# Building the stacked queries and keys of an attention: copies on chip in place of a store and a read

## The reference

```
def _L0_xattn_ref(x1, x2, Wq, bq, Wk, bk, Wv, bv):
    q = proj(x1t, Wq, bq)        # 8 heads of 16 values, 512 positions
    k = proj(x2t, Wk, bk)
    v = proj(x2t, Wv, bv)
    scores = jnp.einsum('bhqd,bhkd->bhqk', q, k) / jnp.sqrt(16)
    attn = jax.nn.softmax(scores, axis=-1)
    out = jnp.einsum('bhqk,bhkd->bhqd', attn, v)
...
x = x + jnp.tanh(g_xattn[0]) * _L0_xattn_ref(_layernorm(x, axis=-1), ctx_2048, ...)
x = x + jnp.tanh(g_ffn[0]) * _L0_ffn_ref(_layernorm(x, axis=-1), ...)
```

## Time and profile before

| | us |
|---|---|
| median of 3 runs | 1391.8 |
| lowest and highest run | 1387.26, 1391.97 |
| the profiled execution, and its span | 1386.7, 1384.8 |
| attention turns, first exact scores to the last values | 51.84 to about 877 |

### The profile page before, as it was taken

One profiled execution on the slowest core, in us unless ns is written; L12 is line 12 of the kernel. 1 busy time (PEld: TensorE's weight loads), 2 busy tenths in 40 slices (PEclk: granted clock), 3 DMA queues, 4 the chain that ended last, 5 costly groups with the idle time before them and its releaser, 6 DMA issues.

```text
span 1384.8 us, 34397 instructions
## 1 busy us (share of the span) xinstructions
PE 1288.3 (93%) x12274; PEld 682.2 (49%) x12274; DVE 975.1 (70%) x1661; ACT 871.8 (63%) x1720; POOL 861.5 (62%) x1267
## 2 busy tenths in 40 slices
PE   2899999999999999999999989799999999999997
PEld 0233333333333333333333323587788888888886
DVE  5989889999999998989999877457654333333332
ACT  2488888888888888888888768333334333333332
POOL 8647777678787878877887643442114555555553
PEclk7799999999999999999999999999999999999999
DMA  7677887778888888788888773676555998885665
GB/s 187 185 197 227 224 241 220 207 227 214 201 223 207 213 218 227 191 222 210 218 217 221 162 185 90 161 161 149 127 175 105 214 216 193 178 189 110 108 110 81
DMA packets 167522, 256.65 MB, mean 185 GB/s; under 512 B 31717, under 2 KB 65132, under 8 KB 167358
## 3 DMA queue, kind: packets, MB, share of 16 engines
q1 hardware_dynamic: 149102, 217.08, 59.0%
q0 software_dynamic: 18256, 37.38, 14.9%
HBM read 141.06 MB, written 112.27 MB: 183 GB/s over the span
## 4 chain that ended last, share of the span: by engine, by line
PE 61%; DVE 12%; issue 10%; DMA 7%; POOL 3%; ACT 3%; SPq 2%; POOLq 1%; DVEq 0%; ACTq 0%
PE m_banks L956 21%; PE bank L913 12%; PE bank L882 10%; DVE row_max L1129 8%; PE m_banks L860 7%; PE bank L838 3%; PE bank L888 3%; DMA arena<-parts_q 2%; PE bank L844 2%; ACT arena L1413 2%; DMA arena<-ht_d 1%; POOL xs L780 1%; PE bank L978 1%; SPq L458 1%; PE bank L869 1%
## 5 line engine op out<-in xcount | busy, mean ns | idle before, releaser
L1129 DVE TENSOR_REDUCE row_max<-m_banks 128x2 f32<-128x1024 f32 x512 | 615.0, 1222 | 76.1 <-PE m_banks L860 67.9
L1413 ACT ACTIVATE arena<-bank 128x512 f32<-128x512 f32 x1024 | 552.4, 606 | 73.4 <-PE bank L882 71.9
L882 PE MATMUL bank<-arena 112*32 112x512 bf16 x4096 | 336.2, 382 | 6.6 <-ACT arena L1413 3.2
L913 PE MATMUL bank<-arena 128*32 128x512 f32 x2048 | 280.2, 598 | 0.4 <-ACT arena L1421 0.3
L882 PEld LDWEIGHTS bank<-arena 112*32 112x32 bf16 x4096 | 114.7, 95 | 266.0 <-ACT arena L1413 132.4
L792 POOL DMA_INDIRECT out<-xs,ids x71 | 112.3, 1582 | 173.4 <-ACT xs L1495 135.7
L860 PE MATMUL m_banks<-arena 48*128 48x512 bf16 x1024 | 177.4, 393 | 39.6 <-DVE row_max L1129 25.7
L956 PE MATMUL m_banks<-w_ring,h_hi 128*128 x568 | 183.0, 403 | 0.0
L1484 ACT ACTIVATE arena<-m_banks 128x256 f32<-128x256 f32 x103 | 39.5, 384 | 186.9 <-PE m_banks L956 186.9
L860 PEld LDWEIGHTS m_banks<-arena 48*128 48x128 bf16 x1024 | 40.4, 93 | 175.2 <-DVE row_max L1129 79.9
L1337 DVE TENSOR_TENSOR arena<-arena,m_banks 128x256 f32<-128x256 f32 x71 | 29.9, 421 | 116.5 <-ACT arena L1484 116.5
(11 more groups left out here) (182 smaller groups left out, 1999.9 us busy)
## 6 DMA issues: line engine op xcount, KB each, us to landing
arena<-parts_k SPq DMA_DIRECT2D x128, 192.0 KB
arena<-parts_q SPq DMA_DIRECT2D x128, 192.0 KB
parts_k<-arena SPq DMA_DIRECT2D x64, 256.0 KB, 6.6
parts_q<-arena SPq DMA_DIRECT2D x64, 256.0 KB, 5.1
pv_d<-arena SPq DMA_DIRECT2D x32, 512.0 KB, 4.3
split_d<-staged SPq DMA_DIRECT2D x30, 512.0 KB, 9.1
w_ring<-split_d SPq DMA_DIRECT2D x60, 256.0 KB, 3.9
arena<-in_w SPq DMA_DIRECT2D x36, 256.0 KB, 8.4
```

The lines of the kernel that those rows point to most:

```text
L882: last = nc.tensor.matmul(out[c, :], k_stack[b % 3][0:SHIFTED, h, kt * P + c.start:kt * P + c.stop], q_stack[b % 3][0:SHIFTED, h, :], star ...
L913: last = nc.tensor.matmul(pv_ps[2 * DH * j:2 * DH * (j + 1), :], v_ones[b % 3][:, kt, GROUP * g + j, :], probs[pair % 3][:, j, :], start=( ...
L1129: nc.vector.reduce_max(pair, m_ps[(STEPS * b + u) // 2 % M_PAIRS], AX_X).then_inc(s_mx, 1)
L1413: nc.scalar.activation(probs[group % 3][:, j, :], bank_of["scores", b, s], ACT.Exp, scale=float(DH) ** -0.5).then_inc(s_exp, 1)
```

## The change

`parts_d`, `write` and `read` are gone. `copy_parts(b, n, part)` copies one part from its tile straight into the stacks: in slot `at` of three, rows base+at, base+at+3, ... (16 partitions, 3 apart) of a stack receive one part of 16 values by 8 heads. Where both halves (`base` 0 and 64) hold the same part for all heads it is one transfer of 128 KB for each half; otherwise even and odd heads (`a`) differ, and it is transfers of 64 KB of four heads each. For one batch that is 10 transfers for keys (HI 4, MID 4, LO 2) and 8 for queries (HI 4, MID 2, LO 2), 6 of them whole. The two heads of a pair in `max_scores` are now neighbours (2j+a), and the reduction on DVE writes its two columns accordingly.

```diff
+SLOTS_OF = (((HI, HI), (HI, MID), (MID, LO)), ((HI, LO), (MID, MID), (HI, HI)))
+COPIES = tuple(sum(2 if first == second else 4 for first, second in slots) for slots in SLOTS_OF)
...
-        parts_d = [[dram(f"parts_{n}{i}", (4, DH, HEADS, L), BF16) for i in range(2)] for n in "kq"]
...
+            def copy_parts(b, n, part):
                 if part == HI:
+                    if n == 0:
+                        if b >= 3:
+                            sp.wait_ge(s_es, STEPS * (b - 2))
+                        if b < 3:
+                            sp.wait_ge(s_blank[b], 2)
                     sp.wait_ge(s_hi, 2 * b + n + 1)
+                if part == MID:
                     sp.wait_ge(s_part, 4 * b + 2 * n + 2)
+                stack, src = (k_stack, q_stack)[n][b % 3], parts[n][part]
+                for at, (first, second) in enumerate(SLOTS_OF[n]):
+                    for base in (0, LANE):
+                        rows = stack[base + at:base + at + STACK - 2:len(SLOTS_OF[n]), :, :]
+                        if part == first == second:
+                            sp.dma_start(rows, src).then_inc(s_cp[n], DMA)
+                        else:
+                            for a in range(2):
+                                if part == (first if base == LANE * a else second):
+                                    sp.dma_start(rows[:, a:HEADS:2, :], src[a:P:2, :]).then_inc(s_cp[n], DMA)
...
             for i in TURNS:
                 if is_b(i + 2):
-                    write(i + 2, 1, HI)
+                    copy_parts(i + 2, 0, HI)
                 if is_b(i):
                     row(i, 1)
...
                 if is_b(i + 2):
-                    if i + 2 > 0:
-                        read(i + 2, 0)
-                    write(i + 2, 1, MID)
-                    if i + 2 == 0:
-                        read(0, 0)
+                    copy_parts(i + 2, 0, MID)
+                    copy_parts(i + 2, 0, LO)
+                    for part in (HI, MID, LO):
+                        copy_parts(i + 2, 1, part)
...
-                if is_b(i + 2):
-                    read(i + 2, 1)
...
-                if is_b(i + 3):
-                    for part in (HI, MID):
-                        write(i + 3, 0, part)
...
# split (POOL) and evacuate (ACT) wait for s_cp[n] in place of s_wr[n]; max_scores (PE) for both s_cp
-                    pe.wait_ge(s_rd[b % 3], READS * DMA * (b // 3 + 1))
+                    for kind in range(2):
+                        pe.wait_ge(s_cp[kind], COPIES[kind] * DMA * (b + 1))
...
-                    rows, h = slice(LANE * a, LANE * a + STACK), GROUP * g + 2 * a + j
+                    rows, h = slice(LANE * a, LANE * a + STACK), GROUP * g + 2 * j + a
```

More of the change, by code:

```diff
@@ L147, in build @@
         held = [a.take(3 * L // 2, BF16).rearrange("p (t l) -> p t l", t=3) for _ in range(2)]
-        parts = [[held[n][:, HELD[n].index(part), :] for part in (HI, MID, LO)] for n in range(2)]
+        parts = [[held[n][:, part, :] for part in (HI, MID, LO)] for n in range(2)]
         wq, wk, wv = (a.take(P) for _ in range(3))
@@ L282, in build @@
         s_part = sem("s_part")
-        s_wr = [sem(f"s_wr{i}") for i in range(2)]
-        s_rd = [sem(f"s_rd{i}") for i in range(3)]
+        s_cp = [sem(f"s_cp{i}") for i in range(2)]
         s_ms = sem("s_ms")
@@ L395, in middle_rows @@
             return stack[LANE // 2:LANE, :, :].rearrange("p h l -> p (h l)").bitcast(F32)
-        def lane(v, a):
-            return v.rearrange("p (g a j) l -> p a g (j l)", g=2, a=2)[:, a, :, :]
         @block.sync
@@ L433, in _ @@
                 load_x(b)
-            def write(b, n, part):
-                if b >= 2 and part == HI:
-                    sp.wait_ge(s_rd[(b - 2) % 3], READS * DMA * ((b - 2) // 3 + 1))
+            def copy_parts(b, n, part):
                 if part == HI:
+                    if n == 0:
[3 more added lines that the diff above has]
+                            sp.wait_ge(s_blank[b], 2)
                     sp.wait_ge(s_hi, 2 * b + n + 1)
-                else:
+                if part == MID:
@@ L667, in split @@
                 pool.wait_ge(s_part, 4 * b + 2 * n)
-                pool.wait_ge(s_wr[n], WRITES * DMA * b)
+                pool.wait_ge(s_cp[n], COPIES[n] * DMA * b)
                 hi, mid, lo = parts[n]
@@ L1127, in maximum @@
                 half, w = divmod(u // 2, GROUP * KT // 2)
-                pair = row_max[b % 2][:, GROUP * KT * half:GROUP * KT * (half + 1)].rearrange("p (a w) -> p w a", a=2)[:, w, :]
+                pair = row_max[b % 2][:, GROUP * KT * half:GROUP * KT * (half + 1)].rearrange("p (j a t) -> p j t a", a=2, t=KT)[:, w // KT, w % KT, :]
                 nc.vector.reduce_max(pair, m_ps[(STEPS * b + u) // 2 % M_PAIRS], AX_X).then_inc(s_mx, 1)
@@ L1394, in evacuate @@
                         act_e.wait_ge(s_part, 4 * (b - 1) + 2 * n + 2)
-                        act_e.wait_ge(s_wr[n], WRITES * DMA * b)
+                        act_e.wait_ge(s_cp[n], COPIES[n] * DMA * b)
                     nc.scalar.activation(proj[n], bank_of["projection", b, n], ACT.Identity, bias=bias[:, n:n + 1]).then_inc(s_evac, 1)
```

## The result

The changed kernel takes 1400.7 us (median of 9 runs) where the kernel before takes 1392.0 beside it: a ratio of 1.0067, 95% interval 1.0038 to 1.0097 (the two medians alone give 1.0063). Forecast were 14 us less. A gain "on the changed kernel" is the quotient of two such ratios.

What follows compares the result with a forecast made beforehand. The prediction took a turn as a tight weave of PE, DVE and ACT, with PE idle time ending in transfers to win. Start 4, turns 10 and m_rows 0 made 14 us less: 1378 us against the median 1391.8, range 1362 to 1398.

Steps and rivals of the forecast that it cites:

- Start: Kernel's start: first maxima 6.4 us earlier, first exact scores from 51.84 to 47.5; 4 us gained, bounds 1 and 6.4.
- The stalls on `parts_q`: In the turns: ten stalls of the maxima's scores waiting for query parts end; 10.0 us gained.
- Issue of the copies: SP's queue: 0.62 us a copy, 18 copies 11.2 us, 3.8 us more each turn, covered by SP's own waits.
- that rival: SP becomes the bound: copies cost over 0.86 us to issue, PE starts turns late; 1417 us at 0.95; chance 0.12.
- The wait for the reciprocals: SP's queue: the reciprocals' load directly follows their store, a new wait of 2.5 us a turn.
- `m_rows`: Exact scores' waits for the rows of maxima, 3.9 us before: taken as 0 change, bounds gain 3.9 and loss 5.
- DMA engines: DMA share of a turn falls from 0.85 to 0.69 by bytes; no gain booked.

Runs made afterwards that it cites:

- e8: Changed kernel, the reciprocals' load reading as many bytes from input x instead, so SP needn't wait for their store; ratio 0.9819 to the kernel before.
- e10: Kernel before, with the reciprocals' store moved behind the four query reads, directly ahead of the load that waits for it; ratio 1.0311 to the kernel before.
- e12: Changed kernel, reciprocals' store ahead of the queries' MID copy and DVE's moments at slot 15 instead of 10; 1377.6 us, ratio 0.9888 to the kernel before.
- e1: Changed kernel, with the last four query copies (MID, LO) moved behind the store of the reciprocals; ratio 0.9947 to the kernel before.
- e11: Changed kernel, with the store of the reciprocals moved ahead of the queries' MID and LO copies; ratio 0.9946 to the kernel before.
- e14: Changed kernel, POOL splitting the queries before adding the attention, and DVE's moments at slot 15 instead of 10; ratio 0.9960 to the kernel before.
- e15: Changed kernel, with the load of pv_d issued before the wait for the reciprocals instead of after it; ratio 0.9933 to the kernel before.
- e4: Changed kernel, with DVE's moments of the attention's output at slot 15 of a turn instead of 10; ratio 0.9974 to the kernel before.
- e9: Changed kernel, with each copied part going to 16 neighbouring partitions instead of every third; ratio 1.0173 to the kernel before.
- e2: Changed kernel, same 18 copies a batch, each carrying 64 of 512 positions, stacks filled beforehand; ratio 1.0026 to the kernel before.

## Why the prediction was wrong, by its own steps

- **Start: right in mechanism, 4 us forecast, 5.5 measured.** First maxima forecast at 25.0, seen at 24.58; first exact scores at 47.5, seen at 46.38. Two sizes were off in opposite directions: the row was issued at 43.91 instead of 43.1, and the PE started 1.3 us after its issue ended (45.12), so it landed in under 3.8 us.
- **The stalls on `parts_q`: right that they end, too much booked for them.** None is left. But the 10.0 us for the turns came from the waits of the weight loads, which run beside the matmuls. The PE's own waits for `parts_q` in the kernel before were smaller, and 6.5 of them lie at the start, so 6.7 in four turns are left:

```profile
PE m_banks L860 <- DMA arena<-parts_q: 13.2, 5, 6.5
```

- **Issue of the copies: near.** 0.62 us forecast; 0.62 to 0.70 in the groups of the turn shown, and 1.1 for the first whole copies after the turn's start (two in 2.21 us, from 332.54); the mean over 526 copies between 60 and 850 us is 0.74. The point from which it was to decide, 0.86, wasn't reached, and the kernel was slower nonetheless: that rival's cover counted only the PE as the one who waits, and only the copies as what makes the row late.
- **The wait for the reciprocals: size right, price wrong.** 2.5 us a turn forecast, 63.7 / 31 = 2.1 measured. This is the step that failed: the wait stands in the working, and nothing in the sum. I let SP reach the end of its turn in time: the keys' HI copies were to be out by 357.9, ahead of `row(i, 1)` at 359.21. They went from 358.89 to 362.55, and the row at 362.60. I also didn't ask who waits for the loads behind the wait. It is POOL, which I had set aside with "POOL isn't the bound", although its 86.9 us of waits for `pv_d` stood in the earlier trace rows. POOL is no bound by its busy time, but DVE's moments wait for its sum, and the PE for the maxima behind them. e8 puts the wait's price at 2.5% of the changed kernel, e10 at 3.1% of the kernel before.
- **`m_rows`: 0 forecast, bounds −3.9 and +5; 13.0 us more of waits measured**, outside the bounds. The lateness of the row was computed for one turn in which everything else keeps its place. Forecast was 2.4 us; in the turn shown `row(i+1, 0)` goes at 351.38, 5.6 us before the next turn's start, where it went at 344.97, 10.2 us before: 4.6 us later, and most of the 3.3 us of cover is gone.
- **DMA engines: right.** No gain was booked for the lower share, and none is seen; it fell from 0.79 to 0.60 between 60 and 850 us, somewhat more than the forecast 0.85 to 0.69 of one turn. The Trainium skill's rule against many small transfers ("DMA: Bandwidth & Descriptors", section "Rules for kernel authors") would have turned the change down. The changed kernel is slower, but these runs put that down to the order in the queue: e8 and e12 keep all 18 copies and are 1.8% and 1.1% faster than the kernel before.
- **DVE's moments** (L1073) weren't in the working at all. They sit in the middle of the maxima's queue and wait for POOL: 32.8 us.
- **The granted clock** wasn't either. Stalls of the PE were counted by their length; five times in these turns the clock fell as well, and the PE was busy 7.0 us longer for the same work.

What stays open: how the 34 us between e8 and the changed kernel divide among SP's lateness for the PE (`m_rows`) and POOL's for DVE. e8 also loads other data and waits for nothing, e1 and e11 change more than one order, e14 gave no verdict, and e15 shortens SP's wait together with POOL's. e4 alone gives a part by itself: moving DVE's moments, with SP's order untouched, brings back 0.9%. The clock's share is open too.

## What to carry to other kernels

Between a store and the load that waits for it, whatever an in-order queue issues is cover; before transfers are taken from there, ask what the load's consumer does next, not only when the queue is free again. An engine far from its bound by busy time can still close a loop that runs once a turn: follow its output once around, add up landings and waits, and compare the sum with the turn. In e10 a wait of 3.5 us in such a loop (106.4 us in 30 turns) cost 3.1%, and in e1 four transfers put back into the gap gave 1.2%, where 1.0% was all that the change was forecast to gain. And count a stall of the PE with what the granted clock does after it.

## What the runs showed that was not expected

The same 18 copies took 70% instead of 60% of the DMA engines' time when their 16 destination partitions were neighbours instead of three apart (e9 and the changed kernel; 165 and 168 GB/s in the same stretch). And the issue of a copy hardly depends on its bytes. With an eighth of them (e2) eight copies in a turn took SP 5.93 us, against 5.63 in the changed kernel's turn shown above, and the means over the turns are 0.73 and 0.74 us a copy:

```profile
334.45 5.93 SPq L446 DMA_DIRECT2D arena<-arena  x8
```
